# Row-maximum scores from rounded high parts, two heads in the two row halves of the array; one causal mask moved to VectorE, the other made fp32r

## The reference

```
q  = x @ Wq           # 32 heads of 32;  kv = x @ Wkv  (ONE key head and one value head, 32 each)
s  = q . k * 32**-0.5 + slope[head] * (kpos - qpos),   -inf where kpos > qpos
x1 = layernorm(x + softmax(s) @ v @ Wo)
out = layernorm(x1 + x1 @ W.T + b + low-rank update chosen per token by a gate)
```

## Time and profile before

| | us |
|---|---|
| median of 3 runs | 4210.84 |
| lowest, highest | 4203.0, 4215.06 |
| span of the profiled execution | 4202.6 |
| PE busy | 3850.6 (92%) |
| DVE busy | 2472.1 (59%) |
| ACT busy | 1929.4 (46%) |
| POOL busy | 1359.6 (32%) |

### The profile page before, as it was taken

The page is one execution under the profiler, slowest core; times in us unless marked ns, Lnnn a source line. Parts: engine busy times, 40 slices in busy tenths (PEclk is TensorE's granted clock), DMA queues, the critical chain, the costliest instruction groups (busy, mean ns, idle before and its releaser), DMA issues. The chain is left out here.

```text
span 4202.6 us, 73921 instructions
## 1 busy us (share of the span) xinstructions
PE 3850.6 (92%) x22065; PEld 2340.6 (56%) x22065; DVE 2472.1 (59%) x4462; ACT 1929.4 (46%) x3253; POOL 1359.6 (32%) x420
## 2 busy tenths in 40 slices
PE   5989989999999998789999999999999599999998
PEld 3555544444444443555554444544443388888887
DVE  4566666666766672556666656766675244444444
ACT  2445645565666565344555656566565401000000
POOL 1114434444444454112433444445454200000010
PEclk8899989999999998899998999999998799999999
DMA  2111110000000001111001000000000311111111
GB/s 72 47 51 27 28 41 22 20 21 16 19 19 14 19 6 34 54 44 49 26 26 43 19 22 22 14 19 14 19 14 6 131 56 60 60 60 60 60 60 51
DMA packets 159069, 152.11 MB, mean 36 GB/s; under 512 B 8388, under 2 KB 141508, under 8 KB 156584
## 3 DMA queue, kind: packets, MB, share of 16 engines
q1 hardware_dynamic: 158696, 147.70, 11.9%
HBM read 96.75 MB, written 33.62 MB: 31 GB/s over the span
## 5 line engine op out<-in xcount | busy, mean ns | idle before, releaser
L509 ACT ACTIVATE prob<-ps_s,alibi 128x512 f32<-128x512 f32 (+3 forms) x2560 | 1524.5, 623 | 1193.3 <-PE ps_s L774 603.4
L589 DVE TENSOR_REDUCE mxp<-ps_a 128x1 f32<-128x512 f32 (+3 forms) x2560 | 1457.6, 605 | 910.2 <-PE ps_a L707 462.5
L452 POOL TENSOR_TENSOR prob<-prob 128x2048 f32<-128x2048 f32 (+1 forms) x240 | 1043.8, 4349 | 1298.2 <-ACT prob L509 1298.2
L771 PE MATMUL ps_s<-qst,kexp 97*128 97x512 f32 (+3 forms) x2560 | 1107.2, 444 | 84.8 <-ACT prob L509 52.8
L771 PEld LDWEIGHTS ps_s<-qst,kexp 97*128 97x128 f32 x2560 | 504.1, 198 | 905.9 <-ACT prob L509 710.4
L707 PE MATMUL ps_a<-kmax,qst 97*128 97x512 f32 (+3 forms) x2560 | 950.3, 397 | 29.2 <-DMA qst<-qst 13.4
L794 PE MATMUL ps_o<-prob,val 128*32 128x512 f32 (+3 forms) x5120 | 624.8, 562 | 0.0
L707 PEld LDWEIGHTS ps_a<-kmax,qst 97*128 97x128 f32 x2560 | 503.3, 197 | 107.6 <-DVE mxp L589 52.7
L794 PE MATMUL ps_sum<-prob,ones 128*32 128x512 f32 (+3 forms) x3200 | 384.8, 569 | 0.1
L980 POOL TENSOR_TENSOR hb_sb<-h_sb,bias_b 128x1024 f32<-128x1024 f32 x32 | 76.9, 2402 | 790.9 <-DVE z_sb L1124 731.1
L607 DVE RECIPROCAL r_sb<-s_sb 128x128 f32<-128x128 f32 x256 | 233.8, 931 | 122.0 <-ACT s_sb L515 119.8
(11 more groups left out here) (148 smaller groups left out, 3672.5 us busy)
## 6 DMA issues: line engine op xcount, KB each, us to landing
wq_raw<-in_L_attn_Wq SPq DMA_DIRECT2D x65, 512.0 KB, 3.8
xs<-in_L_attn_hidden_states SPq DMA_DIRECT2D x9, 2048.0 KB, 8.1
qst<-qst SPq DMA_DIRECT2D x64, 256.0 KB
att_scratch<-at_sb SPq DMA_DIRECT2D x64, 256.0 KB, 2.3
at_raw<-att_scratch SPq DMA_DIRECT2D x32, 512.0 KB, 5.4
x_sb<-in_L_attn_hidden_states SPq DMA_DIRECT2D x32, 512.0 KB, 4.3
out<-z_sb SPq DMA_DIRECT2D x32, 512.0 KB, 3.1
z_sb<-in_L_attn_Wo SPq DMA_DIRECT2D x4, 512.0 KB, 5.3
```

The lines of the kernel that those rows point to most:

```text
L452: nc.gpsimd.tensor_tensor(even[:, :, c1:], even[:, :, c1:], odd[:, :, c1:], ALU.add).then_inc(pair_done, 1)
L509: nc.scalar.activation(prob[slot][:, h, c0:], ps_s[bank][:, c0:], ACT.Exp, bias=alibi_of(u, h, k - QT * s)).then_inc(e_done, 1)
L589: nc.vector.tensor_reduce(mxp[:, h * QT + t, c:c + 1], ps_a[bank][:, 0:cols], AX.X, ALU.max).then_inc(a_done, 1)
L771: last = nc.tensor.matmul(ps_s[bank][:, c0:], kexp[0:KR, k * P:(k + 1) * P], qst[buf][0:KR, h, c0:], start=True, stop=not diagonal)
```

## The change

The A scores are made from the rounded high parts alone: 32 rows of high parts and one row of slope times key position, 33 rows in place of 97. Heads are taken in pairs: `qpair` holds the even heads in rows 0 to 32 and the odd ones in rows 64 to 96, `kmax` the keys in the same two places, and the two matmuls of a pair are issued one behind the other, into two of the three banks. The list of A steps has half as many entries, of two tiles each. The A mask matmul goes; on the diagonal VectorE's maximum becomes one instruction that adds an fp32 mask (`maska`, in SBUF), writes the sum back to the bank and keeps the maximum. The S mask stays a matmul, with fp32r operands. SyncE issues five copies a unit for the stack in place of two.

```diff
 def a_chunks(s):
-    return [(h, t, c, ...) for c in range(s + 1) for h in range(GH) for t in range(QT)]
+    return [(pr, t, c, ...) for c in range(s + 1) for pr in range(2) for t in range(QT)]
...
+        qpair = [sb(ctx, f"qpair{i}", [P, 2, QB], F32R) for i in range(3)]
...
             def put_slopes(b, s, u, buf, old_tiles):
...
-                sp.dma_start(last_row(buf), rows).then_inc(stack_in, 16)
+                for e in range(2):
+                    at = 2 * DH * e + DH
+                    sp.dma_start(qpair[buf][at:at + 1].bitcast(F32), rows[e]).then_inc(stack_in, 16)
             def repeat_q(b, s, u, buf):
...
+                for e in range(2):
+                    at = 2 * DH * e
+                    sp.dma_start(qpair[buf][at:at + DH].bitcast(F32),
+                                 high.rearrange("p (h e) t -> p e h t", e=2)[:, e]).then_inc(stack_in, 16)
...
-            def maximum(tiles, i, chunk, bank):
+            def maximum(tiles, i, chunk, s, before):
+                pr, t, c, cols = chunk
+                for e in range(2):
+                    ps = ps_a[bank_of(before + 2 * i + e)][:, 0:cols]
+                    out = mxp[:, (2 * pr + e) * QT + t, c:c + 1]
+                    dve.wait_ge(a_full, tiles + (2 * i + e + 1))
+                    if c < s:
+                        nc.vector.tensor_reduce(out, ps, AX.X, ALU.max).then_inc(a_done, 1)
+                    else:
+                        dve.sem_inc(went_on, 1)
+                        nc.vector.tensor_tensor_reduce(ps, ps, maska[:, QB - cols:QB], 1.0, MASKED, ALU.add, ALU.max,
+                                                       out).then_inc(a_done, 1)
...
             def scores_for_max(...):
-                pe.wait_ge(a_done, tiles + (0 if first and i < 3 else i - 2))
-                last = nc.tensor.matmul(ps[:, 0:cols], qst[buf][0:KR, h, t * P:(t + 1) * P],
-                                        kmax[0:KR, c * QB:c * QB + cols], start=True, stop=c < s)
-                if c == s:
-                    last = nc.tensor.matmul(ps[:, cols - P:cols], identb[:], maskb[:], start=False, stop=True)
-                last.then_inc(a_full, 1)
+                pe.wait_ge(a_done, tiles + (0 if first and i == 0 else 2 * i - 1))
+                for e in range(2):
+                    rows = slice(2 * DH * e, 2 * DH * e + DH + 1)
+                    nc.tensor.matmul(ps_a[bank_of(before + 2 * i + e)][:, 0:cols],
+                                     qpair[buf][rows, pr, t * P:(t + 1) * P],
+                                     kmax[rows, c * QB:c * QB + cols], start=True, stop=True).then_inc(a_full, 1)
...
-                            last = nc.tensor.matmul(ps_s[bank][:, c0:c0 + P], identb[:], maskt[:], ...)
+                            last = nc.tensor.matmul(ps_s[bank][:, c0:c0 + P], identr[:], masktr[:], ...)
```

More of the change, by code:

```diff
@@ L91, in a_chunks @@
 def a_chunks(s):
-    return [(h, t, c, QB if c < s else (t + 1) * P) for c in range(s + 1) for h in range(GH) for t in range(QT)]
+    return [(pr, t, c, QB if c < s else (t + 1) * P) for c in range(s + 1) for pr in range(2) for t in range(QT)]
 Q_SPACE = 0.5
@@ L183, in attention @@
     with ExitStack() as ctx:
-        identb = sb(ctx, "identb", [P, P], BF16)
-        maskb = sb(ctx, "maskb", [P, P], BF16)
-        maskt = sb(ctx, "maskt", [P, P], BF16)
+        identr = sb(ctx, "identr", [P, P], F32R)
+        masktr = sb(ctx, "masktr", [P, P], F32R)
+        maskt = sb(ctx, "maskt", [P, P], F32)
+        maska = sb(ctx, "maska", [P, QB], F32)
         ones = sb(ctx, "ones", [P, DH], F32)
@@ L355, in put_slopes @@
                 sp.wait_ge(s_full, START + old_tiles)
-                sp.wait_ge(stack_in, START + 32 * g)
-                rows = slope_rows[bass.ds(u * GH, GH)].rearrange("(a h) t -> a h t", a=1)
-                sp.dma_start(last_row(buf), rows).then_inc(stack_in, 16)
+                sp.wait_ge(stack_in, START + STACK * g)
+                rows = slope_rows[bass.ds(u * GH, GH)].rearrange("(a h e) t -> e a h t", a=1, e=2)
+                for e in range(2):
+                    at = 2 * DH * e + DH
+                    sp.dma_start(qpair[buf][at:at + 1].bitcast(F32), rows[e]).then_inc(stack_in, 16)
             def repeat_q(b, s, u, buf):
@@ L419, in _ @@
             nc.gpsimd.iota(dist_i[:], [[P, DIST0 + QT]], base=-P * DIST0, channel_multiplier=1).then_inc(pool_c, 1)
-            pool.wait_ge(pool_c, 6)
-            nc.gpsimd.iota(kpos_i[3 * DH:KR], [[1, T]], base=0, channel_multiplier=0).then_inc(pool_c, 1)
+            pool.wait_ge(pool_c, 5)
+            for at in (DH, 3 * DH):
+                nc.gpsimd.iota(kpos_i[at:at + 1], [[1, T]], base=0, channel_multiplier=0).then_inc(pool_c, 1)
             pool.wait_ge(pool_c, 7)
[L423 to L426, removed]
+            nc.gpsimd.affine_select(out=ident[:], in_=ident[:], compare_op=ALU.not_equal, fill=1.0, base=0,
+                                    pattern=[[-1, P]], channel_multiplier=1).then_inc(pool_c, 1)
+            last = maska[:, QB - P:QB]
+            nc.gpsimd.affine_select(out=last, in_=last, compare_op=ALU.is_ge, fill=MASKED, base=0,
                                     pattern=[[-1, P]], channel_multiplier=1).then_inc(pool_c, 1)
@@ L531, in _ @@
             nc.vector.tensor_copy(dist[:], dist_i[:]).then_inc(vec_c, 1)
-            nc.vector.tensor_copy(kmax[3 * DH:KR], kpos_i[3 * DH:KR]).then_inc(vec_c, 1)
-            dve.wait_ge(vec_c, NH + 3)
+            for at in (DH, 3 * DH):
+                nc.vector.tensor_copy(kmax[at:at + 1], kpos_i[at:at + 1]).then_inc(vec_c, 1)
+            dve.wait_ge(pool_c, 10)
+            nc.vector.tensor_copy(identr[:], ident[:]).then_inc(vec_c, 1)
+            nc.vector.tensor_copy(masktr[:], maskt[:]).then_inc(vec_c, 1)
+            dve.wait_ge(vec_c, NH + 6)
             slope4_c = slope4[:].rearrange("p h t -> p (h t)")
@@ L570, in take_kv @@
                 dve.wait_ge(kv_lo, START + sg + 1)
-                nc.vector.tensor_copy(kmax[0:3 * DH, cols], kexp[0:3 * DH, cols].bitcast(F32)).then_inc(kv_done, 1)
+                for at in (0, 2 * DH):
+                    nc.vector.tensor_copy(kmax[at:at + DH, cols], kexp[at:at + DH, cols].bitcast(F32)).then_inc(kv_done, 1)
             def take_v(b, s):
@@ L615, in prologue @@
                 for i, chunk in enumerate(a_chunks(0)):
-                    maximum(START + b * TILES_B, i, chunk, bank_of(i))
+                    maximum(START + b * TILES_B, i, chunk, 0, 0)
                 take_q(b * UB + 1, 1)
@@ L632, in step @@
                     if what == "A":
-                        maximum(tiles + GH * ktiles(s), i, arg,
-                                bank_of(tiles_before(*ahead(s, const, 1, const)) + i))
+                        s1, u1 = ahead(s, const, 1, const)
+                        maximum(tiles + GH * ktiles(s), i, arg, s1, tiles_before(s1, u1))
                         i += 1
@@ L648, in _ @@
         def _(pe):
-            pe.wait_ge(pool_c, 11)
+            pe.wait_ge(pool_c, 10)
             pe.wait_ge(vec_c, NH)
@@ L698, in project_q, with scores_for_max @@
                     last.then_inc(q_ps, 1)
-            def scores_for_max(g, tiles, first, s, i, chunk, buf, bank):
-                h, t, c, cols = chunk
-                ps = ps_a[bank]
+            def scores_for_max(g, tiles, first, i, chunk, buf, before):
+                pr, t, c, cols = chunk
                 if i == 0:
-                    pe.wait_ge(stack_in, START + 32 * (g + 1))
-                pe.wait_ge(a_done, tiles + (0 if first and i < 3 else i - 2))
-                last = nc.tensor.matmul(ps[:, 0:cols], qst[buf][0:KR, h, t * P:(t + 1) * P],
-                                        kmax[0:KR, c * QB:c * QB + cols], start=True, stop=c < s)
-                if c == s:
-                    last = nc.tensor.matmul(ps[:, cols - P:cols], identb[:], maskb[:], start=False, stop=True)
-                last.then_inc(a_full, 1)
+                    pe.wait_ge(stack_in, START + STACK * (g + 1))
+                pe.wait_ge(a_done, tiles + (0 if first and i == 0 else 2 * i - 1))
[4 more added lines that the diff above has]
+                                     kmax[rows, c * QB:c * QB + cols], start=True, stop=True).then_inc(a_full, 1)
             def turn_shift(g):
@@ L751, in step @@
                     if what == "A":
-                        scores_for_max(g + 1, tiles + GH * ktiles(s), False, ahead(s, 0, 1, const)[0], i, arg,
-                                       parity(s, const + 1),
-                                       bank_of(tiles_before(*ahead(s, const, 1, const)) + i))
+                        scores_for_max(g + 1, tiles + GH * ktiles(s), False, i, arg, parity(s, const + 1),
+                                       tiles_before(*ahead(s, const, 1, const)))
                         i += 1
@@ L773, in step @@
                         if diagonal:
```

(2 more changed lines are left out.)

24 lines of the change are left out of this document (10 added, 14 removed).

## The result

The changed kernel takes 5033.62 us (median of 5, 5003.45 to 5046.86) against 4210.84 (4203.0 to 4217.3): ratio 1.1947, 95% interval 1.1911 to 1.1983. The direction was as forecast; the size, 823 us, is ten times the 80 forecast, and far outside the range of 4060 to 4400.

What follows compares the result with a forecast made beforehand. PE was taken to set the pace in all segments. PE sum 53, S mask 0, shift wait 19, ring 5, clock 5, prologues 2 made +84 us, put as +80 on the median: 4290 us, range 4060 to 4400.

Steps and rivals of the forecast that it cites:

- rival 3: The two matmuls of an A pair do not run side by side: +246 us, 4536 us; chance 0.06.
- S to pair, pair to S, and behind that S: PE's starts around a pair at 512 columns: 0.32, 0.43 and 0.34 us expected.
- rival 1: Division changes cost nothing: about 3880 us, or 4075 if the edge stays; chance 0.27 together, 0.1 for 3880.
- The removal alone: Masks and second A matmuls leaving PE save 376 us; new changes of division give it all back.
- The masked maximum's price: On VectorE, 0.690 us plus 0.083 for its accumulator read, and 0.05 for an extra semaphore instruction.
- The PE sum: On PE, pairs between full-array matmuls +97 us, ahead of sums -5, diagonal ones ahead of sums -39: +53.
- The clock: In attention, PE streams fewer columns and waits longer at L715, so more time at the lower level: +5 us, 0 to +60.
- The ring: In the three A banks, other VectorE work between pairs can make PE wait up to 0.5 us: +5, 0 to +60.
- rival 2: The ring binds: PE waits at most pairs for DVE, some +80 us more, 4370 us; chance 0.12.
- The shift wait: At L715 the shift comes 0.4 us later in 48 units of segments 1 to 3: +19 us, bounds 0 and +70.
- The A mask's removal: On the diagonal, an A tile averages 0.275 us with its bf16 mask and 0.16 without; 1024 masks go.
- The fp32r S mask: On PE, one more 128-column matmul of 0.11 us; between -40 and +40 us over 1024, taken as 0.

Runs made afterwards that it cites:

- 12, 128 rows: Kernel before's tile-by-tile order with both mask changes, A from the high parts alone, zero-filled to 128 rows on the full array: 4215.72 us.
- 10: Changed kernel with each matmul of a pair reading all 128 rows, zeros in the other head's rows, one behind the other: 4410.88 us.
- 2: Changed kernel with 64 rows in each half in place of 33, the added rows zeros: 4592.21 us.
- 9: Changed kernel with 64 rows in each half, plain maximum over the first 128 columns in place of 512: 4462.06 us.
- 11: Changed kernel with pairs on the full array, plain maximum over the first 128 columns of 512: 4342.27 us.
- 12, 65 rows: Kernel before's tile-by-tile order with both mask changes, A from the high parts alone, zero-filled to 65 rows: 4314.08 us.
- 1: Kernel before with only both mask changes: A mask added in VectorE's maximum, S mask in fp32r; 4207.41 us.
- 6: Kernel before with only the A mask moved into VectorE's maximum: 4188.74 us with 97 rows, 4149.39 us with 128 rows in both sets of scores.
- 7: Kernel before with both mask changes and 128 rows in both sets of scores: 4173.58 us.

## Why the prediction was wrong, step by step

The runs build a ladder from the kernel before to the changed one:

| from, to | us | difference |
|---|---|---|
| before, to high parts with both mask changes, full array, tile by tile (12, 128 rows) | 4211 to 4216 | +5 |
| to the order in pairs and its ring (10) | 4411 | +195 |
| to row halves with 64 rows (2) | 4592 | +181 |
| to 33 rows: the changed kernel | 5034 | +441 |

The first step has several changes in it that cancel (masks, high parts, 128 rows for 97 in A). The clock is in all the others: the time at 1.2 GHz goes from 532 us (12) to 633 (10), 1085 (2) and 2251. So some 50 us at most of the second step and up to 226 of the third can be the clock's, and only in the fourth is the row count the one thing changed. Between 10 and 2 the rows of a matmul go from 128 to 64, the array is divided, and PE streams fewer columns; which of these took the clock down there was not separated.

**What held.** PE sets the pace. The two matmuls of a pair run side by side (rival 3 fell). Each step from start to start came as written with 33 rows as with 64: S to pair, pair to S, and behind that S (rival 1 fell). The removal alone did not make it faster. The masked maximum's price was right within 0.03 us. That "slower" came true is in part luck: the sum that gave it, +53 for PE, is a small part of the loss.

**The PE sum: +53 us.** At full clock it was of the right size. A unit of segment 3 goes from full array to halves, both in pairs, by this:

```profile
1177.70:1249.90 72.20, 65.47 (x373) 32.09 (x369) 47.92 (x92) 44.11 (x71) 34.51 (x9) 1.00 0.08 20
```
```profile
1648.30:1721.90 73.60, 67.29 (x373) 27.46 (x369) 47.55 (x91) 44.26 (x71) 34.44 (x9) 1.00 0.08 19
```

(experiment 10, then 2): +1.4 us. By the forecast's own steps it should be some 4 there (18 x 0.16 - 6 x 0.03 for the full pairs, and on the diagonal 5 x 0.23 and 3 x 0.04, as both have no mask to lose). A change in place costs 0.14 to 0.15 (55 more changes, 99 for 44, less the 6.8 us of second matmuls that go). That part of each edge was already there as short stalls, so that PE's baseline was not 0.23 from each matmul to the next, fits but is not shown. The error is on the safe side and small.

**The clock: +5 us, bounds 0 and 60.** This is the step that failed. The prediction let the clock move by a per cent or two, with the columns PE streams and its wait at L715, and gave the rows of a matmul no price at all. The clock fell to 0.775, and 441 us hang on the row count alone. The prediction looked at where the clock fell (behind the shift wait) but not at what brings it back: before, PE's next matmuls had 97 and 128 rows, and behind the 3.5 us of the earlier trace rows the clock was back:

```profile
1462.80:1466.00 3.20, 3.20 (x41) 2.03 (x41) 0.11 (x1) 1.31 (x4) 0.29 (x1) 1.00 0.31 90
```

With 33-row pairs among them it stayed at 1.2 GHz for up to 82 us at a time. Whether it is the rows of each matmul that count, or the share of the array in use over a stretch, no run separates. The Trainium skill, "TensorE: Matmul & The Clock Gate", Terms, speaks of a monitor that watches PE's busy-ness. By busy time alone experiment 2, and 65 for 128 rows in experiment 12, should have changed nothing; the traces differ, and the measurement decides.

**The ring: +5 us, bounds 0 and 60, and as rival 2 +80.** Mis-sized too: the order in pairs costs 195 us on the full array. PE's waits for the maxima were 11 us before, 25 tile by tile (12, 128 rows) and 138 there. The slack was reckoned as time between pairs less VectorE's work, 0.5 us; but a stall shorter than a matmul's tail (0.16 us, the 0.39 that it is shown long less the 0.23 to the next start) does not show as idle time in the profile, so the 11 us of before were no sign that there was slack. Such a stall stands in the timeline of experiment 10, PE's rows:

```profile
1501.43 0.51 PE L798 MATMUL ps_s<-qst,kexp 97*128 97x512 f32 x1 [0.26 <-ACT prob L525]
1501.91 0.72 PE L738 MATMUL ps_a<-kmax,qpair 128*128 128x512 f32 x2
```

The pair starts 0.48 us after S where 0.34 would do, and no idle time is put down to it. Experiments 9 and 11 put 130 (a part of it the clock's) and 69 us on the plain maxima alone. At full clock a unit of segment 3 goes from 67.8 (12, 65 rows) to 72.2 us (10), so in the 16 units of segment 3 alone an estimated 70 of the 195 us are there without the clock.

**The shift wait: +19 us.** Wrong in sign: 100.4 us before, 63.1 after. With PE slower, VectorE is ready sooner. Where the clock stayed high the wait grew a little: 110.2 with both masks alone (1), 104.7 in pairs (10).

**The masks.** The A mask's removal was priced at 0.12 a mask and is worth some 25 us in all, with 97 rows as with 128 (6); in a unit of segment 3 at full clock it is 1.1 us and not 1.9 (1). Where the rest goes is open. The fp32r S mask, taken as 0 within 40, costs 19 to 24 us (7).

**The range** reached up to 4400 because each unknown had been bounded from rows in which A had 97 rows. No row of before shows a stage in which many matmuls use few rows, and the bound should have been open on that side.

## What to carry to other kernels

Before packing small matmuls into row halves among full-array ones, count the changes of division (here 0.14 to 0.2 us each) and ask what the granted clock will see: with many 33-row matmuls TensorE stayed at 1.2 GHz for up to 82 us while PE was busy for 99% of them. Where a contraction is shorter than the array, filling it with rows of zeros costs no time at full clock (a unit of segment 3 is 67.8 us with 65 rows and 68.0 with 128) and raised the clock here (33 to 64: -441 us; 65 to 128: -98 us; 97 to 128 in both sets: -0.8%). And when tiles are issued in groups, look first whether the ring is deep enough for the group: three banks hold one and a half pairs, and the order in pairs cost 195 us here. A deeper ring was not tried.

## What the runs showed of the hardware

- The granted clock depends on the number of rows that the matmuls and their weight loads name, and not on data in them alone: with zeros in all added rows, clock 0.775 to 0.882 (33 to 64 rows in the halves), 0.910 to 0.937 (65 to 128 rows in A), 0.949 to 0.962 (97 to 128 in A and S).
- Added work can shorten a kernel: 1280 full-array matmuls more took 195 us off; 1280 more pairs of 33 rows added 301 us.
- Two row halves run side by side: a pair of 512 columns is as long as a single matmul (0.50 us), in fp32r.
- A row of zeros more or less (64 or 65) decides whether the array is divided: 5365 against 4314 us, and 81.7 against 67.8 us for a unit at full clock.
